# Attention scores from two fp32 parts on two halves of TensorE's rows

## What is computed

```python
h = _layernorm(x) * (1 + ca) + sa
q, k, v = split(einsum('bnd,ed->bne', h, w_in))            # 16 heads of 16
scores = where(causal, -inf, einsum('bhqd,bhkd->bhqk', q, k) * 16 ** -0.5)
out = einsum('bhqk,bhkd->bhqd', softmax(scores), v)
x = x + ga * (einsum('bnd,ed->bne', out, w_out) + b_out)
h = _layernorm(x) * (1 + cb) + sb
# xr, xk: h mixed with the h of the token before
x = x + gb * (sigmoid(xr @ W_r.T) * (square(relu(xk @ W_k.T)) @ W_v.T))
```

## Time and profile before

| | us |
|---|---|
| median of 3 runs | 1738.19 (1734.22 to 1741.68) |
| profiled execution, its time | 1726.74 |
| its span | 1725.1 |
| mean granted TensorE clock | 0.947 of 2.4 GHz |

### The profile page before, as it was taken

One profiled execution on the slowest core, in us unless ns is written; L12 is line 12 of the kernel. 1 busy time (PEld: TensorE's weight loads), 2 busy tenths in 40 slices (PEclk: granted clock), 3 DMA queues, 4 the chain that ended last, 5 costly groups with the idle time before them and its releaser, 6 DMA issues.

```text
span 1725.1 us, 33029 instructions
## 1 busy us (share of the span) xinstructions
PE 1449.8 (84%) x10024; PEld 755.3 (44%) x10024; DVE 1180.8 (68%) x2306; ACT 911.7 (53%) x1795; POOL 734.0 (43%) x876
## 2 busy tenths in 40 slices
PE   3798998788998988989898888978889789889754
PEld 2353344344543444444453444434454344544343
DVE  4668676867677776777668675787757777677342
ACT  2056655655555555565545655555545655565612
POOL 2213314454353533555344543444445453344456
PEclk9789999999998999899998999999999999999968
DMA  3211122111311122111211113111122112211100
GB/s 104 55 63 49 48 78 74 57 39 56 100 64 35 52 69 88 56 53 51 96 51 49 46 57 101 55 38 50 57 91 69 41 44 68 70 57 49 50 33 25
DMA packets 101873, 102.98 MB, mean 60 GB/s; under 512 B 21296, under 2 KB 89912, under 8 KB 101696
## 3 DMA queue, kind: packets, MB, share of 16 engines
q1 hardware_dynamic: 98176, 91.59, 16.4%
q0 software_dynamic: 2560, 8.39, 1.3%
q10 hardware_dynamic: 960, 0.79, 0.2%
HBM read 31.74 MB, written 8.94 MB: 24 GB/s over the span
## 4 chain that ended last, share of the span: by engine, by line
PE 48%; DVE 21%; issue 12%; ACT 9%; POOL 5%; SPq 2%; DMA 2%; DVEq 1%; ACTq 0%; POOLq 0%
PE row_ps L1073 9%; PE val_ps L1097 9%; PE col_ps L1043 8%; PE dense_ps L1107 7%; DVE max_a L868 7%; PE dense_ps L1109 5%; PE dense_ps L1108 5%; ACT weights L712 4%; DVE mixed L981 3%; PE row_ps L1078 2%; DVE max_b L868 2%; PE dense_ps L1126 2%; DVE xn_c L907 1%; SPq L458 1%; DVE gated L965 1%
## 5 line engine op out<-in xcount | busy, mean ns | idle before, releaser
L712 ACT ACTIVATE weights<-col_ps 128x512 f32<-128x512 f32 (+1 forms) x1216 | 620.9, 580 | 473.0 <-PE col_ps L1043 470.9
L868 DVE TENSOR_REDUCE max_a<-row_ps 128x1 f32<-128x512 f32 (+3 forms) x864 | 550.3, 663 | 238.3 <-PE row_ps L1078 155.3
L1073 PE MATMUL row_ps<-k_stack,q_stack 96*128 96x512 bf16 (+3 forms) x1536 | 469.8, 344 | 51.6 <-DVE max_a L868 33.3
L1043 PE MATMUL col_ps<-q_stack,k_stack 99*128 99x512 bf16 (+3 forms) x1536 | 400.8, 337 | 54.0 <-ACT weights L712 33.8
L594 POOL TENSOR_SCALAR_AFFINE_SELECT weights<-weights 128x512 f32<-128x512 f32 x256 | 171.0, 668 | 543.2 <-ACT weights L712 541.1
L1097 PE MATMUL val_ps<-weights,v_ones 128*32 128x512 f32 (+3 forms) x3072 | 337.0, 511 | 16.7 <-POOL weights L594 16.1
L1073 PEld LDWEIGHTS row_ps<-k_stack,q_stack 96*128 96x128 bf16 x1536 | 146.7, 100 | 354.4 <-DVE max_a L868 168.1
L868 DVE TENSOR_REDUCE max_b<-row_ps 128x1 f32<-128x384 f32 (+3 forms) x352 | 213.2, 635 | 115.0 <-PE row_ps L1078 114.7
L1043 PEld LDWEIGHTS col_ps<-q_stack,k_stack 99*128 99x128 bf16 x1536 | 133.5, 99 | 221.3 <-ACT weights L712 138.3
L1078 PE MATMUL row_ps<-causal,ident_bf 128*128 128x128 bf16 x1024 | 207.4, 227 | 0.0
L1078 PEld LDWEIGHTS row_ps<-causal,ident_bf 128*128 128x128 bf16 x1024 | 104.4, 102 | 14.8 <-issue 0.5
(11 more groups left out here) (127 smaller groups left out, 2251.6 us busy)
## 6 DMA issues: line engine op xcount, KB each, us to landing
q_stack<-q_part SPq DMA_DIRECT2D x384, 64.0 KB, 2.5
k_stack<-k_part SPq DMA_DIRECT2D x372, 64.0 KB, 2.5
xa<-in_x SPq DMA_DIRECT2D x8, 1024.0 KB, 6.6
att<-val_out SPq DMA_DIRECT2D x64, 128.0 KB
recips<-recip_rows SPq DMA_DIRECT2D x32, 256.0 KB
xq<-in_x SPq DMA_DIRECT2D x28, 256.0 KB, 3.0
out<-xq POOLq DMA_DIRECT2D x28, 256.0 KB, 2.6
q_stack<-max_rows SPq DMA_DIRECT2D x192, 4.0 KB
```

The source lines that it names most:

```text
L712: nc.scalar.activation(weights[:, t % 2, h:h + n, 0:q1 - q0], col_ps[bank][:, 0:n * (q1 - q0)].rearrange("p (h q) -> p h q", h=n), ACT.Exp ...
L868: nc.vector.reduce_max(dest, bank[:, 0:len(heads) * (k1 - k0)].rearrange("p (h k) -> p h k", h=len(heads)), AX_X).then_inc(max_done, 1)
L1043: last = nc.tensor.matmul(col_ps[bank][:, i * (q1 - q0):(i + 1) * (q1 - q0)], k_stack[s % 2][:, h, P * j:P * (j + 1)], q_stack[s % 2][:, h ...
L1073: last = nc.tensor.matmul(bank[:, n * width:(n + 1) * width], q_stack[stack][0:ROWS, h, P * i:P * (i + 1)], k_stack[stack][0:ROWS, h, k0:k ...
```

## The change

Queries and keys are split into two rounded fp32 parts (type F32R) in place of three bf16 ones. Three products are stacked: 48 rows, and with two rows for the maximum 50. Such a stack fits in 64 partitions, so that heads 0 and 2 of a group lie on partitions 0 to 63 and heads 1 and 3 on 64 to 127 (`ROW_TILE`). A matmul of the first uses the upper half of the array's rows, one of the second the lower half, and the two are issued as a pair into two banks. At widths 512 and 384 a bank still holds one head, at 256 and 128 it now holds two: 40 column units and 40 row units. The mask of the diagonal also works on half of the rows, in two matmuls of 128 and 64 columns for each head. The maxima are split in two parts (two VectorE operations in place of four), turned by one fp32 matmul and placed by 4 DMAs. VectorE writes the second part of queries and keys itself, and GpSimd's two operations on them are gone. `recept` and `k_relu` share memory with `mix_out` and `h2_diff`; `recept` therefore waits for `out_done`. The number of rows taken in each step is changed, and the first row pair of a step stands after its first column pair at the latest. The fill DMAs keep their number (12 per half) and size (64 KB) and move runs of 2 KB in place of 1 KB.

```diff
-Q_PARTS = (0, 0, 0, 1, 1, 2)
-K_PARTS = (0, 1, 2, 0, 1, 0)
+Q_PARTS = (0, 0, 1)
+K_PARTS = (0, 1, 0)
 ROWS = len(Q_PARTS) * HD
-MROWS = 3
-FILL = 2 * len(Q_PARTS) * 16
+MROWS = 2
+ROW_TILE = 64
+FILL = 2 * 2 * len(Q_PARTS) * 16
+PLACED = 2 * MROWS * 16
...
-COL_HEADS = [{1: 4, 2: 2, 3: 1, 4: 1}[(q1 - q0) // P] for q0, q1, _ in COL_STEPS]
-COL_FIRST = [sum(G // n for n in COL_HEADS[:t]) for t in range(STEPS + 1)]
+def bank_heads(width):
+    return ((0, 2), (1, 3)) if width <= QT else ((0,), (1,), (2,), (3,))
...
-PER_STEP = [2, 3, 3, 3, 3, 4, 4, 5, 5, 4, 2, 1]
+PER_STEP = [2, 4, 2, 4, 5, 4, 4, 4, 4, 4, 2, 2]
...
-        q_stack = [sb(f"q_stack{i}", [ROWS + MROWS, G, N], BF16) for i in range(2)]
-        q_parts = [sb(f"q_part{i}", [P, N], BF16) for i in range(3)]
-        qk_rest = sb("qk_rest", [P, HALF])
+        q_stack = [sb(f"q_stack{i}", [P, 2, G // 2, HALF], F32R) for i in range(2)]
+        q_parts = [sb(f"q_part{i}", [P, N], F32R) for i in range(2)]
...
-        recept = sb("recept", [P, 2, D])
-        k_relu = sb("k_relu", [P, KC, QT])
+        recept = mix_out
+        k_relu = h2_diff
...
-                hold(parts_done, b * 8 + (8 * (s // 4) + 4 * (s % 4 // 2) + 2 * (half + 1)))
-                lo = 64 * (s % 2)
+                hold(free["qk"], b * 8 + (8 * (s // 4) + 4 * (s % 4 // 2) + 2 * (half + 1)))
...
-                        sp.dma_start(stack[buf][HD * r:HD * (r + 1), :, cols],
-                                     parts[part][lo:lo + 64, cols]).then_inc(stack_filled[buf][half], 16)
+                        for odd in range(2):
+                            at, lo = ROW_TILE * odd + HD * r, 64 * (s % 2) + 32 * odd
+                            sp.dma_start(stack[buf][at:at + HD, half].bitcast(F32),
+                                         parts[part][lo:lo + 32, cols].bitcast(F32)
+                                         ).then_inc(stack_filled[buf][half], 16)
...
+            def place_max(stack, half):
+                for part in range(MROWS):
+                    for odd in range(2):
+                        row, lo = ROW_TILE * odd + ROWS + part, 8 * (2 * part + odd)
+                        sp.dma_start(stack[row:row + 1, half].rearrange("p g n -> p (g n)").bitcast(F32),
+                                     max_rows[half][lo:lo + 8, :].bitcast(F32)).then_inc(max_placed[half], 16)
...
-                    wait(act, free["value"], q)
+                    wait(act, out_done, q)
...
-                nc.vector.tensor_scalar(parts[:, :, 0:G], src, -1.0, None, ALU.mult).then_inc(max_chain, 1)
+                hi, lo = (parts[:, 16 * part:16 * part + 16].rearrange("p (g i) -> p i g", g=G)
+                          for part in range(MROWS))
+                nc.vector.tensor_scalar(hi, src, -1.0, None, ALU.mult).then_inc(max_chain, 1)
                 dve.wait_ge(max_chain, chain + 1)
-                nc.vector.scalar_tensor_tensor(max_rest[:], src, -1.0, parts[:, :, 0:G], ALU.mult,
-                                               ALU.subtract).then_inc(max_chain, 1)
-                dve.wait_ge(max_chain, chain + 2)
-                nc.vector.tensor_copy(parts[:, :, G:2 * G], max_rest[:]).then_inc(max_chain, 1)
-                dve.wait_ge(max_chain, chain + 3)
-                nc.vector.tensor_tensor(parts[:, :, 2 * G:3 * G], max_rest[:], parts[:, :, G:2 * G],
-                                        ALU.subtract).then_inc(max_split, 1)
+                nc.vector.scalar_tensor_tensor(lo, src, -1.0, hi.bitcast(F32), ALU.mult,
+                                               ALU.subtract).then_inc(max_split, 1)
...
-                    nc.vector.tensor_tensor(qk_rest[:], dense_flat,
-                                            side[0][:, HALF * half:HALF * (half + 1)],
+                    nc.vector.tensor_tensor(side[1][:, cols], dense_flat, side[0][:, cols].bitcast(F32),
...
+                pair = COL_HEADS[t][c - COL_FIRST[t]:c - COL_FIRST[t] + 2]
+                for i in range(len(pair[0])):
+                    for odd, heads in enumerate(pair):
+                        bank, ago = bank_of(COLS * s + c + odd, COLS * G)
+                        if i == 0:
+                            wait(pe, exp_done, exp_index(b, s, c + odd) + (1 - ago))
+                        rows = slice(ROW_TILE * odd, ROW_TILE * odd + ROWS + MROWS)
+                        last = nc.tensor.matmul(col_ps[bank][:, i * (q1 - q0):(i + 1) * (q1 - q0)],
+                                                stack_at(k_stack[s % 2], rows, heads[i], P * j, P * (j + 1)),
+                                                stack_at(q_stack[s % 2], rows, heads[i], q0, q1),
+                                                start=(i == 0), stop=(i == len(heads) - 1), skip_group_check=True)
+                        if i == len(heads) - 1:
+                            last.then_inc(cols_ready, 1)
...
+            def row_bank(b, s, u):
                 number, ago = bank_of(UNITS * ((s + 1) % G) + u, UNITS * G)
-                bank = row_ps[number]
+                wait(pe, max_done, unit_index(b, s, u) + (1 - ago))
+                return row_ps[number]
+            def turn_max(b, s, u):
+                half = int(u == MT1)
+                bank = row_bank(b, s, u)
+                pe.wait_ge(max_split, b * (2 * G) + (2 * (s + 1) + half + 1))
+                nc.tensor.transpose(bank[:, 0:P], max_parts[half][:].bitcast(F32), ident[:]).then_inc(rows_ready, 1)
+            def row_pair(b, s, u):
                 if u in (0, FIRST_HALF):
                     pe.wait_ge(stack_filled[(s + 1) % 2][int(u > 0)], (b * 2 + ((s + 1) // 2 + 1)) * FILL)
...
+                banks = [None, None]
+                for n in range(len(pair[0])):
+                    for odd, heads in enumerate(pair):
+                        if n == 0:
+                            banks[odd] = row_bank(b, s, u + odd)
+                        rows = slice(ROW_TILE * odd, ROW_TILE * odd + ROWS)
+                        end = n == len(heads) - 1 and not diagonal
+                        last = nc.tensor.matmul(banks[odd][:, n * width:(n + 1) * width],
+                                                stack_at(q_stack[stack], rows, heads[n], P * i, P * (i + 1)),
+                                                stack_at(k_stack[stack], rows, heads[n], k0, k1),
+                                                start=(n == 0), stop=end, skip_group_check=True)
+                        if end:
+                            last.then_inc(rows_ready, 1)
+                for n in range(len(pair[0])) if diagonal else ():
+                    for a in range(2):
+                        for odd in range(2):
+                            rows = slice(ROW_TILE * odd, ROW_TILE * (odd + 1))
+                            end = n == len(pair[0]) - 1 and a == 1
+                            last = nc.tensor.matmul(banks[odd][:, (n + 1) * width - P + ROW_TILE * a:(n + 1) * width],
+                                                    mask_ident[rows, a, :], mask_fill[rows, a, ROW_TILE * a:P],
+                                                    start=False, stop=end, skip_group_check=True)
+                            if end:
+                                last.then_inc(rows_ready, 1)
...
-                        while state[1] < min(total, (total * state[0] + work // 2) // work):
-                            row_unit(b, s, next(rows))
+                        while state[1] < min(total, max(1, (total * state[0] + work // 2) // work)):
+                            u = next(rows)
+                            if ORDER[u] == "mt0":
+                                turn_max(b, s, u)
+                            else:
+                                row_pair(b, s, u)
```

151 lines of the change are left out of this document (60 added, 91 removed).

## The result

The changed kernel took **1921.51 us** (median of 4 runs, 1904.18 to 1933.34) against 1737.72 us of the kernel before (4 runs, 1734.22 to 1741.68): **1.1024 times the time, 95% interval 1.092 to 1.1127**. The forecast was 1708 us, its range ended at 1820 us.

What follows compares the result with a forecast made beforehand. It took about a quarter of the steps as VectorE-bound, most others as bound by TensorE's order with short bank waits. Terms -37 + 16 - 9 = -30 us gave 1708 us; range 1635 to 1820 us, the forecast's own 1675 to 1729.

Steps and rivals of the forecast that it cites:

- What bounded the kernel before: Whole kernel: a quarter of the steps bound by VectorE, most others by TensorE's order with short waits for banks.
- the bound with loads in a row: Score pairs: if a pair's two loads follow each other, no pair under 0.22 us; gain 5.4 us a group, not 7.5.
- halves not side by side: Rival, score matmuls: the halves run serially, 4.7 us a group added, 87 us on the path, 1825 us; chance 0.12.
- Entry into scores after dense work: First score matmul after a dense unit: 0.2 us more, 0.09 for the array's part, 0.11 for the unhidden fp32 load.
- How much shows: Score steps: of 5.3 us a group net TensorE gain, 1.2 us shows, 37 us in all.
- -37 + 16 - 9: Sum in us: shown TensorE gain 37, loss to order and loads after waits 16, VectorE saving that counts 9; -30.
- the column pair behind it starts some 0.3 us later: Eighth step of a third group: row pairs around the first column pair delay the next; about as much saved after the values.
- The clock rival: Rival: shorter score streams leave TensorE idler, two more low-clock stretches in seven batch elements, 77 us, 1785 us; chance 0.21.
- Full gain: Rival: TensorE's saved time counts in full by the scores' 58% share of the chain, 99 us, 1639 us; chance 0.14.
- cancelled: Rival: banks and reductions bound nearly everywhere, saved time turns into waits, gain and added changes cancel, 1738 us; chance 0.17.
- What would show it: Signs: paired starts, score waits growing in total, matmuls' chain share falling, clock near 0.95; under 0.90 favours the clock rival.
- VectorE and GpSimd: VectorE gains 38 us, 9 us of it counting in the quarter it bounds; GpSimd loses 64 operation pairs, no bound.

Runs made afterwards that it cites:

- e2: Changed kernel with both score matmuls of a pair, and their masks, on the lower 64 rows, one after the other: 2216.86 us, 1.2744 times the kernel before.
- e1: Changed kernel with each score matmul and mask on all 128 rows, so nothing runs side by side: 1794.16 us, 1.0346 times the kernel before.
- e6: e1 with the units, table and single issue of the kernel before, leaving only two fp32 parts on whole rows: 1769.77 us, 1.019 times the kernel before.
- e10: Changed kernel with each half's stack filled up with zero rows to 64, same numbers computed: 1851.21 us, 1.0673 times the kernel before.
- e8: e1 with 66 of the 128 rows in every score and mask matmul, same instructions and columns: 2022.06 us, 1.1629 times the kernel before.
- e14: e5 with the changed kernel's table of rows per step, the turn of maxima left in place: 1828.79 us, 1.0536 times the kernel before.
- e5: Kernel before with only the changed kernel's units, issued singly, rows per step following the old running sum: 1736.28 us, 0.9992 times the kernel before.
- e3: Changed kernel with every score pair of 512 and 384 columns issued twice: 1981.6 us, 1.1405 times the kernel before.

## Why the prediction was wrong

**What bounded the kernel before: right,** and so were the mechanics. The pair of 512 columns was priced at 0.23 us, that of 256 at 0.12 and of 128 at 0.11; the rows above show 0.24, 0.12 and 0.11 to 0.14, with the loads overlapping (the forecast's own sum, not the bound with loads in a row). The Trainium skill's price of a load, 107 ns for 128 columns ("TensorE: Matmul & The Clock Gate", "LDWEIGHTS (loading the stationary operand)"), agrees with the 0.11 from one pair to the next, but two halves pay it once; with loads one behind the other, as I weighed it, a pair would have taken 0.22. The rival *halves not side by side* is dead by the same rows, and by e2.

**Entry into scores after dense work: over-sized.** I had 0.2 us (0.09 for the change of the used part and 0.11 for the load). Measured: 0.09 over the pitch, which is the price of the change alone. The load of 0.11, 1.5 us a group in the sum, isn't seen on top of it, and e1 enters without any surplus.

**How much shows: not wrong in kind.** The forecast had precision and halves at -37 + 16 - 9. e6 shows the two-part numbers alone at +34 us, with VectorE's saving worth nothing. For the halves' gain at equal clock there are estimates only. The base is e1, which has the same order and the same two-part numbers: 58 us over the kernel before, at nearly its clock. By the mean clocks TensorE stood at 1.2 GHz for 746 us in the changed kernel, 492 in e10 and 218 in e1. At e8's price of 0.36 us that makes 188 us of clock for the changed kernel over e1 and 97 for e10. Measured over e1 are 123 and 58, which leaves **some -65 us for the halves in the changed kernel and -39 in e10**. Both have the same halves, so the estimate is no better than the 26 us between them. The sign is that of the forecast, and its size isn't contradicted.

**The step that failed first: the clock was held constant.** The sum has terms for streams, loads, changes of the array's part and waits, and none for what half the rows do to the granted clock. The text says that it "should stay near 0.95". It was 0.805 on average, and by e8 that is priced at some 188 us, more than the whole excess over the kernel before.

**The other step: the order was costed at nothing.** The prediction followed one step, the eighth, in which "the column pair behind it starts some 0.3 us later" and as much is saved, and took the others to be like it. In the third group that step became 1.3 us shorter, 4.52 us against 5.80, and e14 has 4.53 with the table alone: the table gives it four units in place of five, and VectorE fills it before and after.

```profile
1102.02:1106.54 4.52, 4.29 (x23) 2.14 (x22) 4.52 (x10) 2.67 (x6) 0.00 (x0) 1.00 0.18 45
```

The steps that pay for it, the fifth above all and the first two, weren't looked at. The fifth stands at the head of the stretch of the earlier trace rows where VectorE is busy in 15.71 of 19.73 us. The table costs 93 us on the bf16 kernel (e5 against e14), but with the two-part numbers of the changed kernel, units, table and pairs together cost 24 us (e6 against e1). The table in the diff, laid beside windows step by step, would have shown the fuller fifth step.

**The clock rival had the right symptom, and the wrong mechanism and size.** It was named at 0.21 and at 1785 us, with two more low stretches of 5.5 us lost in seven elements each, 77 us, because "shorter score streams with longer waits behind them leave it idler". TensorE's waits for ScalarE fell (83 against 138 us) and its low stretches include ones in which it is never idle. e8 shows that the number of rows by itself costs 228 us. The change itself gave reason to suspect it: it takes a matmul from 96 and 99 rows to 48 and 50 in the earlier trace rows's own columns. But nothing in a trace of before varies the rows, so no row there could price it; an upper bound would have been TensorE at 1.2 GHz in all score stages, which I didn't set. So the range ended 101 us short of the median.

**The other rivals.** *Full gain* and *cancelled* fell with the sign. The waits for banks, for which the second stood, did go on: 186 us against 168 for maxima. The Trainium skill's "PSUM Bottleneck" in "TensorEngine Tiling (Array Packing)" names that limit rightly, but it isn't what the time was lost to.

**What would show it.** The text had the clock under 0.90 as the mark of its rival, and the clock was 0.798 in the profile. Waits that grow were to speak for the forecast: those for maxima grew, those for exponentials fell.

**VectorE and GpSimd.** VectorE's busy time fell by 80 us where 38 were summed; 14 us of the rest are in an operation that the change doesn't touch (`mixed`, 655 to 545 ns each). e6 shows no gain in time from a VectorE with 45 us less to do.

In sum, of some 180 us over the kernel before: 34 for the two-part numbers (e6), 24 for the order with them (e1 against e6), some 188 for the clock and some -65 for the halves, the last two by the estimate above.

## What to carry to other kernels

Matmuls on half of the array's rows were paid in clock here, even with a partner on the other half. When a change takes rows from a matmul, put a price on TensorE at 1.2 GHz before trusting a sum of streams: run the old kernel with fewer rows first. And fill unused rows with zeros, which made no stream longer (two pairs of 256 columns take 0.24 us in the changed kernel and 0.23 in e10; 1916 to 1851 us here, and 1735 to 1727 on the old kernel). Where a table says how much work a step gets, look at every step's fullest engine before moving two units into it; an even count isn't an even load. And judge such a move by the sum of the steps around it, since one longer step can be work that came earlier.

## What the runs showed of the hardware

The clock that TensorE is granted depends on how many rows its matmuls use. With the same 9832 matmuls, 128 rows had 0.94 and 66 rows 0.779, and there was a stretch of 6.89 us under way without a gap at 1.2 GHz. Rows of zeros count as rows in use: a mean of 0.805 to 0.867 with 64 rows a half, 0.933 to 0.948 with 128 for 99. Rows aren't all of it: with the same rows and 2048 more matmuls the clock was 0.87 in place of 0.80 (e3).

Two halves of rows load and stream at once. A pair costs what one matmul does (0.24 us at 512 columns, 0.12 at 256), and 0.11 to 0.14 us at 128 columns, with the fp32 loads of both inside. Going from whole rows to halves costs 0.09 us.
